# The scan stage of a vision Mamba block on one Trainium2 core: projections through memory, six decay buffers, and the splitting and the skip term on TensorE

## The reference

```
xs = stack([x row by row, x column by column, both reversed])          # (4, 4, 192, 1024)
dts, Bs, Cs = split(x_proj_weight @ xs, [6, 16, 16])
dt = softplus(dt_projs_weight @ dts + bias)                            # (.., 192, 1024)
h[l] = h[l-1] * exp(dt[l] * A) + (dt[l] * u[l]) * B[l]                 # 16 states per channel
y[l] = sum over states of h[l] * C[l], + D * u[l]
y = sum of the four directions, each turned back to image order
```

## Time and profile before

| | us |
|---|---|
| median of 3 runs | 3095.22 (3094.96 to 3102.87) |
| the profiled execution | 3110.97 |
| its span, first to last instruction | 3108.9 |
| first scan instruction that is followed without a break, to the last | 79.8 to 1541.6 |
| everything after the scan stage | about 1552 to 3109 |

### The profile page before, as it was taken

One profiled execution on the slowest core, in us unless ns is written; L12 is line 12 of the kernel. 1 busy time (PEld: TensorE's weight loads), 2 busy tenths in 40 slices (PEclk: granted clock), 3 DMA queues, 4 the chain that ended last, 5 costly groups with the idle time before them and its releaser, 6 DMA issues. The chain is left out here.

```text
span 3108.9 us, 33979 instructions
## 1 busy us (share of the span) xinstructions
PE 2521.1 (81%) x9156; PEld 920.0 (30%) x9156; DVE 2223.0 (72%) x3030; ACT 1424.7 (46%) x1949; POOL 1311.6 (42%) x677
## 2 busy tenths in 40 slices
PE   4677677776677766776668689999999889999999
PEld 2111111111111111111124123232232246666766
DVE  4999999999999998999755688787878631111112
ACT  3444544445444444444456147676767522222221
POOL 1788878787788877788751100000000200000000
PEclk9777767777677777777758689999999889999999
DMA  3555555555555555555512603131313400000000
GB/s 88 144 167 165 160 152 166 154 155 159 157 168 162 166 146 152 160 152 163 152 47 80 104 2 43 23 42 24 42 23 42 87 1 6 5 5 5 5 5 10
DMA packets 101755, 286.76 MB, mean 92 GB/s; under 512 B 14878, under 2 KB 19137, under 8 KB 101569
## 3 DMA queue, kind: packets, MB, share of 16 engines
q1 hardware_dynamic: 100506, 284.94, 35.1%
q10 hardware_dynamic: 1102, 0.19, 0.0%
HBM read 239.66 MB, written 25.88 MB: 85 GB/s over the span
## 5 line engine op out<-in xcount | busy, mean ns | idle before, releaser
L528 POOL TENSOR_TENSOR hs<-hs,bc 128x1024 f32<-128x1024 f32 x384 | 900.4, 2355 | 224.9 <-DVE hs L614 224.2
L501 ACT ACTIVATE decay<-decay,a_neg 128x1024 f32<-128x1024 f32 x384 | 440.4, 1148 | 666.2 <-DMA decay<-dt_rows 652.3
L425 PE MATMUL psU<-stack,spread_sel 96*128 96x512 bf16 x768 | 361.1, 487 | 425.0 <-DVE hs L614 346.3
L1446 DVE TENSOR_REDUCE mx<-ps 128x1 f32<-128x512 f32 x864 | 539.3, 682 | 117.7 <-PE ps L1285 112.4
L558 DVE TENSOR_TENSOR psU<-psU,bc 128x512 f32<-128x512 f32 x768 | 514.4, 673 | 25.9 <-issue 13.4
L1421 ACT ACTIVATE P<-ps 128x512 f32<-128x512 f32 x768 | 417.6, 599 | 249.3 <-PE ps L1297 225.2
L614 DVE TENSOR_TENSOR_SCAN hs<-decay,psU 128x512 f32<-128x512 f32 x384 | 464.7, 1210 | 72.6 <-PE psY L387 52.4
L614 DVE TENSOR_TENSOR_SCAN hs<-decay,hs,psU 128x512 f32<-128x512 f32 x384 | 487.5, 1269 | 1.1
L387 PE MATMUL psY<-hs,state_sel 128*32 128x512 f32 x1572 | 401.5, 855 | 23.2 <-DVE Y L571 11.2
L1719 DVE SCALAR_TENSOR_TENSOR acc<-psE,gate,acc 128x192 f32<-128x192 f32 x128 | 53.4, 417 | 448.5 <-PE psE L1619 445.5
L1285 PE MATMUL ps<-ks,qs 96*128 96x512 bf16 x864 | 345.0, 404 | 34.8 <-DMA ks<-qk_parts 24.2
(11 more groups left out here) (237 smaller groups left out, 2280.3 us busy)
## 6 DMA issues: line engine op xcount, KB each, us to landing
decay<-dt_rows SPq DMA_DIRECT2D x388, 512.0 KB
stack<-parts SPq DMA_DIRECT2D x297, 64.0 KB, 5.5
dt_rows<-dt SPq DMA_DIRECT2D x33, 384.0 KB, 7.1
qs<-qk_parts SPq DMA_DIRECT2D x90, 128.0 KB, 6.7
ks<-qk_parts SPq DMA_DIRECT2D x90, 128.0 KB, 7.2
qk_parts<-qparts SPq DMA_DIRECT2D x16, 576.0 KB, 3.7
w<-in_L_ffn_w_dram SPq DMA_DIRECT2D x8, 576.0 KB, 9.9
X<-in_x_dram SPq DMA_DIRECT2D x4, 768.0 KB, 9.7
```

What stands on the lines that cost most here:

```text
L425: pe.matmul(psU[:, q % UR, :], s.spread_sel[:, gg, :], stack[:, ui % 2, j, CH * pos:CH * pos + CH], start=True, stop=True).then_inc(dtu_sp ...
L501: nc.scalar.activation(decay[:, t % DR, :], decay[:, t % DR, :], ACT.Exp, scale=s.a_neg[:, col:col + 1]).then_inc(decay_ready, 1)
L528: pool.tensor_tensor(h, h, bc[:, 2 * p + r, 1, :], ALU.mult).then_inc(hc_ready, 1)
L1446: v.reduce_max(mx[:, slot, u:u + 1], ps1[:, (slot * MAXES + u) % R, :], AX.X).then_inc(max_done, 1)
```

## The change

- **Projections.** `w_b`, `w_c` and the combined `w_dt` go. One weight `w_xd` gives, for both directions of a row or column order at once, 6 rows of dts and 32 rows of B and C (`inputs`, PE). ACT copies them to `xd`; SP stores the B and C rows in DRAM (`keep_xd`) and loads them back repeated over the channels (`load_bc`, [8, 16, 1024] into 128 partitions, 512 KB each, two for each of four slots). This happens in units 4 and 6 of each image, the loads in units 5, 6, 7 and 0 after tiles 2 and 4. The dt weights have 6 rows only (`steps`, PE).
- **No turned copy.** `xt` goes. Where columns are needed, the operand of the matmul or of POOL's product is read with a stride of 32 elements (`turned`). `sum_states` reads `hs` with that stride in the column units, so that Y comes out in image order.
- **Sum in PSUM.** The units are ordered by channel half first (f = ui // 4), so all four directions of a half are summed in `psY`; the skip term is a matmul with a diagonal matrix (`skip`, once for four units) and ACT takes the result with one copy for four units. DVE's `take` goes.
- **Splitting on PE.** The differences are made by `remainder`: identity times dt*u minus identity times the parts, in PSUM; ACT copies the result as bfloat16. POOL's two differences go. One remainder stands in tile 10, for the unit after the next, the other in tile 1 of the unit that follows.
- **Order.** The dt chain is moved from tiles 8 to 11 to tiles 3 to 7 (PE `steps` at t = 3, ACT at t = 5, 6, 7, POOL at t = 4 and 5), all nine moves into `stack` to after tile 2, DR = 6 and HR = 8, four slots for dt in DRAM instead of two.
- **DVE** has per tile what it had: two products and two scans.
- **prepare** makes the small weights instead of the large ones, gives its semaphores back and adds a barrier.

The diff of `scan`, cut to what the argument needs:

```diff
-        HR, DR, UR = 6, 4, 4
+        HR, DR, UR = 8, 6, 4
+        DT_AT = 4
         def order(ui):
-            p, f, r = ui // 4, ui // 2 % 2, ui % 2
+            f, p, r = ui // 4, ui // 2 % 2, ui % 2
+        XD_UNITS = {4: 0, 6: 1}
...
+                def inputs(out, nb, p, c):
+                    for h in range(2):
+                        m = pe.matmul(out, s.w_xd[:, p, h, :], turned(s.X[:, nb, h, :], p)[:, 16 * c:16 * c + 16, :],
+                                      start=(h == 0), stop=(h == 1))
+                def steps(nu, c):
+                    pe.matmul(psP[0:HC, c, :], s.w_dt[BLK * r:BLK * r + R, p, HC * f:HC * f + HC],
+                              xd[BLK * r:BLK * r + R, p, CH * c:CH * c + CH], start=True, stop=True).then_inc(z_proj, 1)
+                def remainder(c, known, ready):
+                    m = pe.matmul(psP[0:HC, c, :], s.ident[0:HC, 0:HC], dtu[:, cs], start=True, stop=False)
+                    for i in range(known):
+                        m = pe.matmul(psP[0:HC, c, :], s.minus_bf[:], parts[:, i, cs], start=False, stop=(i == known - 1))
+                    m.then_inc(ready, 1)
+                def skip(b, f, c):
+                    pe.matmul(psY[0:HC, c, :], s.d_diag[:, f, :], s.X[:, b, f, CH * c:CH * c + CH], start=True, stop=False)
...
                     for j in range(NBLK):
+                        h = hs[:, (ui * TILES + 3 * trip + j) % HR, :]
+                        h = h.rearrange("p (w h) -> p h w", h=HH) if p else h.rearrange("p (h w) -> p h w", h=HH)
                         m = pe.matmul(psY[BLK * j:BLK * j + BLK, c, :], s.state_sel[:, trip, :],
-                                      hs[:, (3 * trip + j) % HR, CH * c:CH * c + CH],
+                                      h[:, 16 * c:16 * c + 16, :], start=False, stop=(trip == SUB - 1 and ui % 4 == 3))
...
                                 pe.matmul(psU[:, q % UR, :], s.spread_sel[:, gg, :],
                                           stack[:, ui % 2, j, CH * pos:CH * pos + CH],
                                           start=True, stop=True).then_inc(dtu_spread, 1)
-                                z_side(q, *unit_ahead(b, ui), n + 2)
-                                bc_side(q, b, ui, n)
+                                if t == 1:
+                                    pe.wait_ge(mid_ready, n * 2 + (c + 3))
+                                    remainder(c, 2, tail_ready)
+                                if t == 3:
+                                    if c == 0:
+                                        pe.wait_ge(xd_ready, nb * 4 + (2 * order(nu)[1] + 2))
+                                    pe.wait_ge(lo_ready, n * 2 + (c + 3))
+                                    steps(nu, c)
+                                if t == 6 and ui in XD_UNITS:
+                                    pe.wait_ge(z_taken, n * 2 + 6)
+                                    inputs(psP[:, c, :], (b + 1) % NB, XD_UNITS[ui], c)
+                                if t == 10:
+                                    if c == 0:
+                                        pe.wait_ge(z_taken, n * 2 + 6)
...
+                                        pe.wait_ge(dtu_ready, n + 3)
+                                        pe.wait_ge(hi_ready, n + 3)
+                                    remainder(c, 1, rest_ready)
                                 if t % 3 == 0:
+                                    if t == 6 and ui % 4 == 0:
+                                        if c == 0:
+                                            pe.wait_ge(y_taken, b * 2 + (ui // 4 + 1 + START))
+                                        skip(b, f, c)
...
+                            if t == 11:
+                                act.wait_ge(stacked[(ui + 1) % 2], in_stack(b, ui + 1))
+                                act.wait_ge(dtu_ready, n + 3)
+                                nc.scalar.copy(parts[:, 0, :], dtu[:]).then_inc(hi_ready, 1)
...
                             sp.wait_ge(scan_done, n * (2 * TILES) + (2 * t + 2 + S0))
                             if t + DR < TILES:
-                                load(ui % 2, t + DR)
+                                load_dt(ui % 4, t + DR)
...
-                            if t in (4, 5, 7):
-                                part = (4, 5, 7).index(t)
-                                sp.wait_ge((hi_ready, mid_ready, lo_ready)[part], n + 2)
-                                stack_up(part, (ui + 1) % 2)
+                            if t == 2:
+                                for part, (ready, each) in enumerate(((hi_ready, 1), (mid_ready, 2), (lo_ready, 2))):
+                                    sp.wait_ge(ready, n * each + 2 * each)
+                                    stack_up(part, (ui + 1) % 2)
+                            if t == 2 and ui in (5, 6, 7, 0):
+                                sp.wait_ge(hc_ready, n * TILES + (TILES + START))
+                                load_bc((ui - 5) % UNITS, (0,))
+                            if t == 4 and ui in (5, 6, 7, 0):
+                                load_bc((ui - 5) % UNITS, (1,))
```

More of the change, by code:

```diff
@@ L198, in _ @@
                 for q in range(2 * K):
[L199 to L207, removed]
+                    k, f = q // 2, q % 2
+                    at, row = D * (k % 2) + HC * f, BLK * (k // 2)
+                    m = pe.matmul(ps[row:row + R, 6 + k // 2, at:at + HC], wdt_rows[:, q, :], s.ident[0:HC, 0:HC],
+                                  start=True, stop=True)
                 m.then_inc(pe_wdt, 1)
@@ L293, in scan @@
         landed = [sem(f"landed{i}") for i in range(DR)]
+        bc_landed = [sem(f"bc_landed{i}") for i in range(4)]
         decay_ready = sem("decay_ready")
@@ new lines, in z_end, with part @@
+                def z_end(n1):
+                    act.wait_ge(z_taken, n1 * 2 + 2)
+                    nc.scalar.activation(soft[:], soft[:], ACT.Exp, scale=-1.0).then_inc(exp_own, 1)
+                    act.wait_ge(exp_own, n1 + 1)
+                    nc.scalar.activation(soft[:], soft[:], ACT.Ln, bias=s.one[0:HC, :]).then_inc(log_ready, 1)
+                def part(i, n1, c, rest, ready):
+                    act.wait_ge(rest, n1 * 2 + (c + 1))
+                    nc.scalar.copy(parts[:, i, CH * c:CH * c + CH], psP[0:HC, c, :]).then_inc(ready, 1)
@@ new lines, in take @@
+                def take(b, f, last):
+                    act.wait_ge(summed, last + SUM0)
+                    nc.scalar.copy(s.Y[:, b, f, :], psY[0:HC, :, :].rearrange("p c l -> p (c l)")).then_inc(y_taken, 1)
+                nc.scalar.preload_act_table_set("natural_log_exp_and_others")
+                for p in range(2):
+                    for c in range(2):
+                        act.wait_ge(xd_proj, 2 * p + c + 1)
+                        nc.scalar.copy(xd[:, p, CH * c:CH * c + CH], (psU if p else psP)[:, c, :]).then_inc(xd_ready, 1)
@@ L494, in _ @@
+                z_end(1)
+                act.wait_ge(stacked[0], STACK_INC)
+                act.wait_ge(dtu_ready, 2)
+                nc.scalar.copy(parts[:, 0, :], dtu[:]).then_inc(hi_ready, 1)
                 with act.Fori(0, NB, 1) as b:
@@ new lines, in _ @@
+                            if t == 3:
+                                for c in range(2):
+                                    part(2, n + 1, c, tail_ready, lo_ready)
+                            if t == 4 and ui % 4 == 0:
+                                take(b if ui else (b + (NB - 1)) % NB, 1 - f, n * SUB)
+                            if t == 5:
+                                act.wait_ge(dtu_ready, n + 2)
+                                act.wait_ge(dt_stored, n * 16 + 32)
+                                z_half(nu, n + 2, 0)
@@ L588, in _ @@
                         n = b * UNITS + ui
[L589 removed]
+                        f, p, r, k = order(ui)
                         product(n, ui, 0, b)
```

386 lines of the change are left out of this document (175 added, 211 removed).

## The result

The changed kernel takes 3242.1 us (median of 4 runs, 3221.37 to 3257.78), the kernel before 3099.05 beside it: ratio 1.0448, 95% interval 1.0365 to 1.0532. It is slower, by some 140 us. The forecast was 3090, and the range to 3245 holds the result only near its edge.

The account below looks back on a forecast made before the run. DVE, busiest engine of the scan stage, was taken as the bound. The scan's terms gave 1437 against 1462 (-25), the opening +20, so 3095 - 5 = 3090 us; likely 3060 to 3120, range 3035 to 3245.

Parts of the forecast that it names:

- the opening: Before the first steady scan: `prepare` matmuls saved, but more loads, copies and remainders ahead of the first spread; +20 (8 to 28).
- tiles: DVE's products and scans in the scan loop stay as they are: 384 tiles at 3.485 us, 1338 us.
- loop's turn: DVE's wait at the start of the next image's pass of the loop stays: 13 us.
- all waits not named: DVE's waits for sums (52) and decay tiles (20) go, except some 5 us left for waits not named.
- `inputs` and skip, unit 4: Tile 6 of unit 4: PE's input matmuls, skip and sums stall DVE 5.3 us, four times: 21 (8 to 36).
- `inputs`, unit 6: The same place in unit 6, without skip: 1 us each, 4 (0 to 20).
- wait in tile 10: PE waits for ACT's `hi`, behind load 11's exponential: 3 us of stall in each of 16 units, 48 (0 to 110).
- stride, at tile 3: Strided reading lengthens PE's sums: 0.5 us at tile 3 of each column unit, 8 (0 to 46).
- 13 for the spread: Of DVE's 99 us of waits in the kernel before, 13 were put down to PE's spread.
- the rival that eight engines become the bound: Transfers on eight engines stay at 158 GB/s and bound each unit: 3234 us, chance 0.18.
- PE's bursts: PE's work between spreads was tested against DVE's 2.9 us beyond the spread; stalls of 21 and 4 us in units 4 and 6.
- the rival that this binds PE: Strided groups of sums take 4.1 us and make PE the bound: 3385 us, chance 0.08.

Follow-up runs that it names:

- the last experiment: The kernel before with dt's rows stored twice, plus eight buffers of states for six and three decay buffers for four: ratio 0.9744, 3024.55 us.

## Why the prediction was wrong

The loop was forecast at 1437 and took 1561.5; the opening and the rest were near. Step by step, in the prediction's own terms:

| term of the scan's sum | forecast | measured |
|---|---|---|
| tiles | 1338 | the same means: 676, 1270, 1208 ns |
| takes | gone | gone |
| loop's turn | 13 | 14.9 |
| all waits not named | 5 | 3.7 |
| `inputs` and skip, unit 4 | 21 (8 to 36) | 24.9 |
| `inputs`, unit 6 | 4 (0 to 20) | 22.0 |
| wait in tile 10 | 48 (0 to 110) | 86.6, with tile 11 |
| stride, at tile 3 | 8 (0 to 46) | 0 |
| `steps` beside the sums, tile 4 | not named | 60.0 |

The measured terms add up to 1550. The other 11 us are what neighbouring instructions no longer overlap (some 0.08 us) where DVE idles, about 120 times, so that it is busy 1348 us of the loop and not 1338, and gaps under 0.1 us. The prediction had no term for this, and its account of the kernel before closed at 1462 by luck: of its 99 us of waits 11.0 lie before the first steady scan, outside of the 1462, as these rows and the 1.21 at 79.83 show. So of its "13 for the spread" only 2.7 stood in the loop.

```profile
75.52 0.70 DVE L558 TENSOR_TENSOR psU<-psU,bc 128x512 f32<-128x512 f32 x1 [8.13 <-PE psU L425]
...
77.92 0.70 DVE L558 TENSOR_TENSOR psU<-psU,bc 128x512 f32<-128x512 f32 x1 [1.70 <-PE psU L425]
```

**Right: what goes.** The takes and the two waits ended, and the reason given (two buffers more, so that DVE needs the sums two tiles later) holds in the kernel before as well: in the last experiment it took the wait for the sums away. That the clock, the DMA share and the rate would not change the bound was right too: the rival that eight engines become the bound gives 3234, within 8 us of the result, by a mechanism that isn't there. With sixteen engines on the decay loads the loop fell by 10 us, and tile 10's gap didn't fall.

**The step that failed: PE's bursts.** "What matters is the bursts", with 2.9 us of slack, was the right test, and it was applied to tile 6 alone. Tile 3 has one too in every unit: a half of `steps` is two records, 1.78, a group of sums 1.93 (2.24 with the stride), the spread 0.5. At the lower clock that is 4.2 to 4.5 us from spread to spread, and with both halves and the third spread 8.9 to 9.5, against 2 x 1.74 + 2.9 + 0.5 = 6.9 that DVE gives: an estimate of 2.0 us from the prediction's own terms, 2.6 with the measured stride. The step "at tile 3 of each column unit" looked at this very place and took from it only the 0.5 us that the stride adds. Measured: 1.9 us in each of 32 units, 60 us, in row units as in column units, and 0.0 with `steps` at t = 4. This is the largest part of the miss. Unit 6 is the same step mis-sized: two `inputs` and the sums were put at 1 us, and took 5.5 each time (22.0 / 4), nearly as much as unit 4 with its skip (6.2).

**The wait in tile 10: right mechanism, right place, size too small.** It was forecast as 16 x 3 = 48; measured are 78.4 at tile 10 and 8.2 at tile 11. Unit 0 has 9.2 us each time (36.8 / 4), units 5 and 7 have 4.0, and three of the ordinary units 0.5 to 1.3 each. With the budget of 8.3 us for the load these follow from how long load 11 took (means of four, from the semaphore's updates in the trace): 18.6 - 8.3 = 10.3 in unit 0, 12.8 - 8.3 = 4.5 in unit 5, 13.5 - 8.3 = 5.2 in unit 7. In unit 6 it took 13.7 and DVE didn't wait; it had lost 5.5 us at tiles 6 and 7, behind the issue of the load, which covers it. So the budget held, the 11 to 13 us put for the load held but for unit 0, and that unit is the term that was too small: 37 us for 12. The step put the two loads of `bc` at "4.7 us at the high rate, 7.8 at the low one". Load 11 took 3.7 to 4.6 us longer behind them in units 5, 6 and 7, and 9.5 in unit 0, than the mean of 9.1 in units 1 to 4; with wide decay loads it took 9 to 13 longer. Why unit 0's load is 5 us later than the others' in the changed kernel, and not with wide loads (16.1 there, beside 15.4 and 17.2), stays open. Two ablations agree on what the wait is worth: 94 us with the copy earlier (68 by the loop), 76 without the `bc` loads (60).

**The sum of the waits.** A gap in the table isn't its price. `steps` later took 60 us of gaps away at tile 4 and shortened the loop by 20, since 45 appeared behind the transfer; the copy earlier took 75 away at tiles 10 and 11, 23 at tile 4, and 33 appeared at tiles 1 and 2. A wait for PE and one for a transfer cover each other. The table says where the time stands, the experiments what it is worth.

**The stride: nothing, as by the lower bound.** The group takes 2.24 us, as forecast from ACT's rate (2.2), and no run shows a loss of time from it. By the Trainium skill, "Advanced Engine Details and Errata", section "SBUF Cachelines", a pattern that touches another line of 16 bytes with each element pays a penalty; the trace agrees for the instruction (2.24 against 1.06 at the upper clock), and the rival that this binds PE, 3385, didn't come.

**The opening: 25.7 for 20 (8 to 28).** The first spread came at 102.05 (74.88 before): ACT's copy L502 waited 21.16 us for the nine moves into `stack`, issued between 66.41 and 75.10 behind six decay loads, and PE's remainder behind it 26.22. Wide loads bring the first scan to 92.7.

**The profiled execution** lies 14 us under the median, and that of the kernel before 12 over its own, so 117 of 143 us are explained by one pair of traces; that the rest is more of the same waits is likely, not shown.

## What to carry to other kernels

Where engines run in an order written by hand, price each stretch between two instructions that the critical engine waits for, everywhere that a piece is put, and not the sum over a unit: PE had time free on average and made DVE wait 107 us in three bursts. Before an instruction is placed behind another, ask what the other waits for: the copy `hi` needed nothing of tile 11, but stood behind its transfer, and two tiles earlier was worth 94 us. And look first at what a buffer more is worth: two more buffers of states let the kernel before ask for its sums two tiles later, at no work (0.9869 to 0.9744, with one decay buffer less), and with its loads on all engines it beat every form of the larger change that was run.

## What the runs showed of the hardware

- **A load whose outermost dimension only repeats was slow.** With wide decay loads (sixteen lines outermost, a median of 4.8 us to landing) the first load of `bc` in a unit (eight equal copies of 16 rows, the same 512 KB) lands after 7.9 to 9.3 us, and the second, issued behind it, after 13.9 to 18.0. A decay load behind both took 13.6 to 17.2 in place of 4.4 to 4.7. As eight transfers of 64 KB, 5.4 to 5.6 us after the first one's issue and 8.3 to 9.3 for the second load, for 3.7 us of SP's time instead of 0.6. Whether the equal copies or their number, eight, make it slow was not tried apart. The Trainium skill, "DMA: Bandwidth & Descriptors", section "Rules for kernel authors", says that a leading broadcast of c copies confines a transfer to at most c engines; with eight copies that is half of the width, and the first load's time, not quite twice the decay load's, agrees.
- **Twice the copies in DRAM, sixteen engines:** in the changed kernel the median decay load lands after 4.8 us in place of 8.8 (the means, with the loads behind `bc`, are 6.9 and 9.7), although the store of dt writes 768 KB for 384. The DMA share rises from 0.54 to 0.70, the rate from 160 to 171 GB/s only: a unit moves 8.2 MB for 7.8 in about the same time, and a packet of 4 KB takes 264 ns on average where it took 215 (packets between 110 and 1450).
- **A float32 matmul that reads with a stride of 128 bytes doesn't gain from the upper clock:** 2.23 us for a group of six records at a granted clock of 1.00 and 2.25 at 0.50, where the contiguous one takes 1.06 or 1.93.
